# Two image streams in strict turn: the next image's first half moved beside the second attention

## The chip, the core and the metric

The kernel runs on one core of one Trainium2 chip. The metric is device time in microseconds: the median of three runs is 4172.8 (4169.99 to 4182.94).

## What is computed

A small vision transformer of two layers, on 64 images of 3 x 224 x 224. Each image becomes 196 patches of 16 x 16 and a class token, 197 tokens of 192 features.

```
h = tokens(x)                                   # patches @ W + b, class token, positions
h = h + attention0(layernorm(h))                # one head, 192 wide: q, k, v, softmax
h = h + ffn0(layernorm(h))                      # 3 experts; the image's mean token picks one (top 1)
h = h + attention1(layernorm(h))                # 12 heads of 16, output projection
h = h + ffn1(layernorm(h))                      # 191 tokens: 192 -> 768 -> gelu -> 192
                                                # first 6 tokens: gated experts ("atoms")
```

Everything is float32. Where the kernel uses the TensorE format fp32r it splits an operand into a high part and a remainder, so that a product of 192 features takes five matmuls.

## The kernel before, in words

**Streams and rounds.** Images go in pairs: stream 0 (A) takes the even image, stream 1 (B) the odd one. Each stream has its own half of PSUM, four banks (L260), and its own SBUF tiles. A round does one pair; there are 32 rounds, of which all but the ends are one hardware loop (`run_stages`, L405).

**Stages.** An image's work is a list of 58 named stages, `STAGES` (L69). In order: q0, v0, s0, p0, o0 (first attention: folded query and key, values, scores, transposed softmax, output), stat2, norm2, turn2 (normalisation: moments on VectorE, reciprocal root on POOL, applied on VectorE, transposed on TensorE, split by ScalarE and VectorE), route (expert's choice), hid0 and out0 (first FFN: three stages of products with gelu on ScalarE, two of output), a third normalisation, qk1 and v1, six max stages and maxT (row maxima of the 12 heads' scores), fourteen att stages (scores transposed, exponential, and at att5, att9 and att13 a group of four heads' output with its division on VectorE), proj, a fourth normalisation, hid1 and out1. The stages x, tok0, tok1 and the first normalisation (`AHEAD`, L68) are done for the next image, within the same list.

**Order.** `MERGE` (L80) is a string of 123 letters that says whose stage comes next: a, b, or r for a seventh part of POOL's regrouping of the pixels. It came from a search, and B begins at stage 38. `merged_order` (L84) makes the list `ORDER` of it. Every engine goes through the same list and takes its part of each stage (`stages` in each engine's block), so the list is the program order of all of TensorE, VectorE, ScalarE, POOL and SP (the DMA issues). Between engines there are semaphores.

**Around the change.** On SP, stage route loads the chosen expert (L473 to L489): W1 with remainders, 1188 KB, into `shared`, 384 KB into `w_last`, biases, and W2, 576 KB. `shared` later takes the stacked keys of the second attention, and qk1 fills it by DMA (L491). maxT sends the maxima by DMA into the stacks (L507). norm4 stores six tokens (L511), out1_1 stores the image from a tile `y` (L520). On TensorE, q0 and o0 use bank 2 of the stream, v0 and the outputs bank 3, s0 bank 0, p0 and route bank 1 (`TURN_BANK`, L106, says where a transposition goes). probs0 and the transposed `turned` lie in the ring of the second attention's exponentials (L231, L232), and the first attention's values in the tile `vals` of the second. `norm_count` (L398) counts the normalisations of a stream in their order.

On ScalarE, the exponentials (L1151, L1202, L1226) and the gelu (L1209) need different activation tables, and the compiler puts an ACT_TABLE_LOAD where the function changes.

Of the kernel before, what the change touches and what calls it, by code (L numbers as in the profile page):

```python
# [24 lines left out]
D = 192  # L25
# [21 lines left out]
RING = 6  # L47
STAGED = 2
# [12 lines left out]
def ffn_stages(n):  # L61
# [44 lines left out]
TURN_BANK = {1: 3, 2: 3, 3: 0, 4: 1}  # L106
# [3 lines left out]
def vit_kernel(nc, x, tok_w, tok_b, cls_tok, pos, attn_w, wg, w1, b1, w2, b2, w_qkv, w_proj, b_proj,  # L110
               fc1_w, fc1_b, fc2_w, fc2_b, gate_pair, atom_in_w, atom_in_b, atom_out_w, atom_out_b,
               balance, out, scratch):
    with ExitStack() as ctx:
# [52 lines left out]
        with ExitStack() as loop:  # L166
# [13 lines left out]
            w2_sb = two("w2_sb", [128, HC, D])  # L180
# [50 lines left out]
            probs0 = [probs[p][0][:, 0, :, :] for p in range(2)]  # L231
            turned = [probs[p][0][:, 1, :, :] for p in range(2)]  # L232
            y = two("y", [R, T, D])
# [164 lines left out]
        def norm_count(n, it):  # L398

            if n == 1:  # L400
                return 1 if isinstance(it, int) and it == 0 else 4 * it - 1
            last = isinstance(it, int) and it == PAIRS - 1
            return 4 * it + {2: 2, 3: 4 - last, 4: 5 - last}[n]
# [27 lines left out]
        def _(sp):  # L431
# [36 lines left out]
            def stages(name, p, it):  # L468
# [4 lines left out]
                if name == "route":  # L473

                    sp.wait_ge(expert_ready[p], it + 1)
# [44 lines left out]
                if name == "out1_1":  # L520
                    sp.wait_ge(out_ready[p], it + 1)
                    img = 2 * it + p
                    sp.dma_start(out[bass.ds(img, 1), NCLS:R].rearrange("o s d -> (o s) d"),
                                 y[p][NCLS - 1:R - 1, 0, :]).then_inc(stored[p], 16)
                    sp.dma_start(out[bass.ds(img, 1), R:SEQ].rearrange("o s d -> (o s) d"),
                                 y[p][0:R - 1, 1, :]).then_inc(stored[p], 16)
# [66 lines left out]
        def _(pe):  # L593
# [82 lines left out]
            def hidden(p, n, j, chunk):  # L676
                for c in (2 * j, 2 * j + 1):
                    last = accumulate(bank[p][HIDDEN_BANK[n][j]][:, (c % 2) * SP_:(c % 2 + 1) * SP_],
                                      swapped(products(tokens(p), chunk(c))))
                last.then_inc(hid_done[p], 1)  # L680
# [12 lines left out]
            def stages(name, p, it):  # L693
                b = bank[p]
                if name == "x":
                    if not isinstance(it, int) or it:
                        pe.wait_ge(logit_ready[0], it)
# [22 lines left out]
                elif name == "q0":  # L720
                    pe.wait_ge(xnT_ready[p], norm_count(1, it))
                    for m in range(2):
                        last = accumulate(b[2][:, m * SP_:(m + 1) * SP_], swapped(products(
                            tokens(p, None, tokT), columns(qk_fold, slice(m * 128, (m + 1) * 128)))))
                    last.then_inc(g_done[p], 1)
                elif name == "v0":
                    if not isinstance(it, int) or it:
                        pe.wait_ge(out_ready[p], it)
                    values(p, it, b[3], attn_wv, tokT)
                elif name == "s0":  # L730
                    pe.wait_ge(g_ready[p], it + 1)
                    for t in range(T):
                        last = accumulate(b[0][0:R, t * SP_:(t + 1) * SP_], swapped(products(
                            tokens(p, None, tokT), columns(xnT[p], slice(t * R, (t + 1) * R)))))
                    last.then_inc(s0_done[p], 1)
                elif name == "p0":
                    pe.wait_ge(p0_ready[p], it + 1)
                    for kt in range(T):
                        for t in range(T):
                            last = t_.transpose(b[1][0:R, kt * SP_ + t * R:kt * SP_ + (t + 1) * R],  # L740
                                                probs0[p][:, t, kt * R:(kt + 1) * R], ident[0:R, 0:R])
                    last.then_inc(p0_turned[p], 1)
                elif name == "o0":
                    pe.wait_ge(p0T_ready[p], it + 1)
                    pe.wait_ge(v_ready[p], 2 * it + 1)
                    for t in range(T):
                        last = accumulate(b[2][0:R, t * D:(t + 1) * D],
                                          [(turned[p][:, kt, t * R:(t + 1) * R], vals[p][:, kt, :, 0:HD])
                                           for kt in range(T)])
                    last.then_inc(o0_done[p], 1)  # L750
                elif name == "route":
                    pe.wait_ge(xsum_ready[p], it + 1)
                    accumulate(b[1][0:R, 0:EXPERTS],
# [7 lines left out]
                elif name[:4] == "out0":  # L761
                    if name == "out0_0":
                        pe.wait_ge(experts_loaded[p], 16 * it + 16)
                        if not (isinstance(it, int) and it == PAIRS - 1):
                            pe.wait_ge(xnT_ready[p], norm_count(1, it + 1))
# [8 lines left out]
                elif name == "v1":  # L774
                    values(p, it, b[0], v_wT, xnT)
                elif name[0] == "max":
                    j = name[1]
                    if j == 0:
                        pe.wait_ge(low_ready[p], 2 * it + 2)
                        pe.wait_ge(stacked[p], 144 * it + 144)  # L780
                        pe.wait_ge(v_ready[p], 2 * it + 2)
# [48 lines left out]
                elif name[:4] == "out1":  # L830
                    hid_out(p, it, 1, int(name[5]), fc2_wT, bias_pair[:, 1, :])
# [39 lines left out]
        def _(dve):  # L871
# [12 lines left out]
            for p in range(2):  # L884
                v.memset(probs0[p][:, :, SEQ:SP_], 0.0)
# [54 lines left out]
            def token_moments(p, it, n):  # L940
                dve.wait_ge(h_ready[p], norm_count(n, it))
                for t in range(T):
                    last = v.bn_stats(stats[p][:, t, :], (h_tok[p] if n == 1 else h_tiles[p])[:, t, :])  # L943
# [7 lines left out]
            def apply_norm(p, it, n):  # L951
                dve.wait_ge(rstd_ready[p], norm_count(n, it))
                for t in range(T):
                    for at, lo in ((0, 0), (D, 128)):
                        last = v.tensor_scalar(xn[p][:, t, at:at + D - lo], (h_tok[p] if n == 1 else h_tiles[p])[:, t, lo:D],  # L955
# [3 lines left out]
            def stages(name, p, it):  # L959
# [15 lines left out]
                elif name[:4] == "turn":  # L975

                    n = int(name[4])
                    dst = (tokT if n == 1 else xnT)[p]
# [6 lines left out]
                elif name == "q0":  # L985
# [4 lines left out]
                        in1=b[2][:, 0:2 * SP_], op0=ALU.mult, op1=ALU.add).then_inc(g_ready[p], 1)  # L990
# [275 lines left out]
```

## Time and profile before

| | us |
|---|---|
| median of 3 runs | 4172.8 |
| profiled execution | 4169.5 |
| its span, first to last instruction | 4167.7 |
| TensorE (PE) busy | 3189.7 (77%) |
| VectorE (DVE) busy | 2134.8 (51%) |
| ScalarE (ACT) busy | 1402.9 (34%) |
| POOL busy | 360.5 (9%) |
| granted TensorE clock, mean | 0.862 |

The chain that ended last goes 47% through PE, 29% through DVE, 8% through DMA, 5% through issue and 4% each through SP's queue and ACT. "Busy" is the sum of an engine's instructions; a clock of 1.0 is full speed. The time in brackets at a timeline row is idle time of that engine just before, with what ended it. A number x12 counts instructions that the view has merged; a float32 product counts as two.

### The profile page before, as it was taken

The page shows a single profiled execution, that of the slowest core. Times are in us where ns is not written, and L with a number is a line of the kernel's source. Part 1 is how long each engine was busy: PE and PEld are TensorE (multiplying, and loading weights), DVE is VectorE, ACT ScalarE, POOL GpSimd, SP SyncE. Part 2 cuts the span into 40 slices and gives each one's busy share as a digit, 9 for nine tenths or more (in the row PEclk, how much of TensorE's full clock was granted, in tenths as well). Part 3 has the DMA queues.
Part 4 walks back from the last instruction along what each step waited for, and adds up shares of the span by engine and source line. Part 5 has one row for each costly group of instructions (what it writes and reads, how often), then busy time and mean ns, then how long its engine had stood idle before and what let it go on. Part 6 is the DMA issues. An engine that isn't in the chain of part 4 may idle for free.

```text
span 4167.7 us, 63512 instructions
## 1 busy us (share of the span) xinstructions
PE 3189.7 (77%) x23190; PEld 2834.1 (68%) x23190; DVE 2134.8 (51%) x5288; ACT 1402.9 (34%) x2904; POOL 360.5 (9%) x746
## 2 busy tenths in 40 slices
PE   4777877777877777777777787777778777777757
PEld 3667766767766676776666776667677666677646
DVE  4555555554555555555555455554555555555433
ACT  2333333333333333333333333333333333333321
POOL 1000000010000000010001000010010000100000
PEclk9888888888988888888888898888888888889877
DMA  4332222332322333222233232223322223322221
GB/s 122 79 80 70 69 60 47 81 79 69 79 57 56 64 79 78 71 70 58 47 81 79 69 81 66 55 54 80 80 69 73 56 47 80 79 73 66 64 62 32
DMA packets 127223, 287.54 MB, mean 69 GB/s; under 512 B 28791, under 2 KB 95368, under 8 KB 116173
## 3 DMA queue, kind: packets, MB, share of 16 engines
q1 hardware_dynamic: 127180, 286.97, 29.7%
q8 instruction: 27, 0.44, 0.0%
q14 instruction: 16, 0.12, 0.0%
HBM read 192.23 MB, written 15.00 MB: 50 GB/s over the span
## 4 chain that ended last, share of the span: by engine, by line
PE 47%; DVE 29%; DMA 8%; issue 5%; SPq 4%; ACT 4%; POOL 3%; DVEq 0%; POOLq 0%; ACTq 0%
PE banks L640 21%; PE banks L687 8%; DVE inv L1061 5%; DVE hx L955 5%; PE banks L817 5%; DMA shared<-low 4%; DVE nmax L1050 4%; PE banks L786 4%; PE banks L804 3%; DMA shared<-nmaxT 3%; DVE stats L943 3%; POOL rstd L586 2%; PE banks L664 2%; DVE xnT L981 2%; DVE sums L1059 2%
## 5 line engine op out<-in xcount | busy, mean ns | idle before, releaser
L786 PE MATMUL banks<-shared,q_stack 128*99 128x198 f32 x1536 | 282.2, 336 | 238.4 <-issue 103.3
L1050 DVE TENSOR_REDUCE nmax<-banks 99x4 f32<-99x788 f32 x384 | 360.3, 974 | 155.8 <-PE banks L786 152.5
L786 PEld LDWEIGHTS banks<-shared,q_stack 128*99 128x99 f32 x1536 | 225.3, 225 | 292.3 <-issue 110.8
L640 PE MATMUL banks<-xnT,fc_wT 128*128 128x198 f32 x1920 | 359.3, 363 | 42.1 <-DVE xnT L981 42.1
L640 PEld LDWEIGHTS banks<-xnT,fc_wT 128*128 128x128 f32 x1920 | 346.0, 278 | 50.1 <-DVE xnT L981 50.0
L804 PE MATMUL banks<-q_stack,shared 128*99 128x198 f32 x1536 | 268.0, 301 | 140.1 <-DMA shared<-nmaxT 118.4
L1191 ACT ACTIVATE xnT<-banks 128x396 fp32r<-128x396 f32 x192 | 96.1, 501 | 820.6 <-PE banks L664 820.6
L584 POOL TENSOR_TENSOR var_eps<-moments,eps 99x2 f32<-99x2 f32 x256 | 51.1, 200 | 3642.2 <-DVE moments L948 3642.2
L804 PEld LDWEIGHTS banks<-q_stack,shared 128*99 128x99 f32 x1536 | 204.4, 194 | 203.6 <-DMA shared<-nmaxT 106.8
L687 PE MATMUL banks<-w_sb,hidT 128*99 128x192 f32 x1536 | 338.7, 383 | 0.0
L955 DVE TENSOR_SCALAR hx<-hx,moments,rstd 99x192 f32<-99x192 f32 (+1 forms) x768 | 248.0, 385 | 160.8 <-POOL rstd L586 157.2
L1226 ACT ACTIVATE probs_first<-banks 99x396 f32<-99x396 f32 x256 | 114.0, 497 | 616.2 <-PE banks L804 616.2
L687 PEld LDWEIGHTS banks<-w_sb,hidT 128*99 128x99 f32 x1536 | 293.2, 201 | 11.7
L687 PE MATMUL banks<-fc_wT,hidT 128*99 128x192 f32 x1536 | 273.0, 327 | 0.0
L640 PE MATMUL banks<-tok_wT,xT 128*99 128x192 f32 x1536 | 270.0, 330 | 3.5 <-ACT xT L1182 0.9
L1061 DVE RECIPROCAL inv<-sums 128x198 f32<-128x198 f32 x192 | 267.2, 1392 | 6.6
L817 PE MATMUL banks<-probs_rest,vals 99*32 99x198 f32 (+1 forms) x2048 | 186.7, 361 | 100.4 <-DVE headT L1063 65.5
L640 PEld LDWEIGHTS banks<-tok_wT,xT 128*99 128x99 f32 x1536 | 245.4, 168 | 8.9 <-issue 7.2
L1226 ACT ACTIVATE probs_rest<-banks 99x396 f32<-99x396 f32 x512 | 228.0, 497 | 64.6 <-PE banks L804 61.3
L687 PEld LDWEIGHTS banks<-fc_wT,hidT 128*99 128x99 f32 x1536 | 240.6, 166 | 0.5
L1209 ACT ACTIVATE hidT<-banks,fc_bc 128x198 f32<-128x198 f32 x384 | 142.5, 423 | 290.3 <-PE banks L640 290.3
L664 PE MATMUL banks<-ident,hx 99*128 99x99 f32 x1024 | 158.0, 284 | 106.2 <-DVE hx L955 103.9
(191 smaller groups left out, 5592.3 us busy)
## 6 DMA issues: line engine op xcount, KB each, us to landing
shared<-w_split SPq DMA_DIRECT2D x64, 1188.0 KB
xin<-in_x_dram SPq DMA_DIRECT2D x32, 1176.0 KB
w_sb<-in_L_ffn_W_dram SPq DMA_DIRECT2D x64, 576.0 KB, 6.2
w_last<-w_split SPq DMA_DIRECT2D x64, 384.0 KB
q_stack<-hi SPq DMA_DIRECT2D x128, 148.5 KB
q_stack<-low SPq DMA_DIRECT2D x128, 148.5 KB
shared<-hi SPq DMA_DIRECT2D x128, 148.5 KB
shared<-low SPq DMA_DIRECT2D x128, 148.5 KB
```

Source lines behind the costliest of these rows:

```text
L640: last = t_.matmul(dst, a, b, start=(j == 0), stop=(j == len(pairs) - 1))
L664: last = t_.transpose(b[:, k * SP_ + t * R:k * SP_ + (t + 1) * R], xn[p][:, t, k * 128:(k + 1) * 128], ident[0:R, 0:R])
L687: t_.matmul(b[0:R, t * D:(t + 1) * D], hidT[p][:, c, t * R:(t + 1) * R], w[:, c, :], start=(c == 0), stop=False)
L786: last = t_.matmul(b[n % 4][0:R, t * SP_:(t + 1) * SP_], q_stack[p][:, n, t * R:(t + 1) * R], k_stack[p][:, n, :], start=True, stop=True)
L804: last = t_.matmul(b[s % 2][0:R, kt * SP_:(kt + 1) * SP_], k_stack[p][:, s, kt * R:(kt + 1) * R], q_stack[p][:, s, :], start=True, stop=True)
L817: last = t_.matmul(b[2][r:r + 32, 0:SP_], vals[p][0:rows, kt, head(h), :], ring(p, h)[0:rows, kt, :], start=(kt == 0), stop=(kt == T - 1))
L943: last = v.bn_stats(stats[p][:, t, :], (h_tok[p] if n == 1 else h_tiles[p])[:, t, :])
L955: last = v.tensor_scalar(xn[p][:, t, at:at + D - lo], (h_tok[p] if n == 1 else h_tiles[p])[:, t, lo:D], moments[p][:, t, 0:1], rstd[p][:, ...
L1050: v.tensor_reduce(nmax1[p][:, :, 2 * j:2 * j + 2].rearrange("p t h -> p h t"), src, AX, ALU.max, negate=True).then_inc(nmax1_ready[p], 1)
L1061: v.reciprocal(inv1[p][:], sums1[p][:]).then_inc(inv1_ready[p], 1)
L1209: last = s_.activation(hidT[p][:, c, :], b[HIDDEN_BANK[layer][j]][:, (c % 2) * SP_:(c % 2 + 1) * SP_], ACT.Gelu, bias=bias[:, c:c + 1], sc ...
L1226: s_.activation(ring(p, s).rearrange("p k s -> p (k s)"), b[s % 2][0:R, 0:T * SP_], ACT.Exp).then_inc(p1_ready[p], 1)
```

## The change

The stages q0 to route of an image move into `AHEAD`: they are done for the next image, q0 and v0 ahead of the max stages and s0, p0, o0, the second normalisation and route between the att stages (`BESIDE`). The expert's load becomes a stage of its own, load, behind proj, since it overwrites `shared`. The order is no longer the searched one: A and B take turns stage by stage, and B begins at stage 28 of 57. The rest follows from that: h of the first half stays in `h_tok` until out0_1, probs0, `turned` and the values `vals0` get tiles of their own (in space of `w2_sb`), the image is stored from `h` in place of `y`, the first half uses bank 3 (v0 bank 1, the first transposition bank 0), the second half of keys takes 98 rows in place of 99, and waits guard what is shared.

```
-AHEAD = ["x", "tok0", "tok1"] + norm_stages(1)
-STAGES = (["q0", "v0", "s0", "p0", "o0"] + norm_stages(2)
-          + ["route", "x", "tok0", "tok1", "stat1", "split", "norm1", "hid0_0", "hid0_1", "turn1",
-             "hid0_2", "out0_0", "out0_1"] + norm_stages(3) + ["qk1_0", "qk1_1", "qk1_2", "v1"]
-          + [("max", j) for j in range(HEADS // 2)] + ["maxT"] + [("att", s) for s in range(HEADS + 2)]
-          + ["proj"] + norm_stages(4) + ffn_stages(1))
-B_FIRST = 38
-MERGE = ("bbbbbabbabbbbabbababbbabaababbbababaaabbaaabababararbaabrbabbbaabrbbarabbrbaaaaa"
-         "aaabaababaaaabaababaaabaaabbabbrabbabaabbab")
+AHEAD = (["x", "tok0", "tok1"] + norm_stages(1) + ["q0", "v0", "s0", "p0", "o0"] + norm_stages(2)
+         + ["route", "load"])
+BESIDE = {1: "s0", 3: "p0", 5: "o0", 7: "stat2", 8: "norm2", 9: "turn2", 11: "route"}
+ATTENTION = []
+for s in range(HEADS + 2):
+    ATTENTION += [("att", s)] + ([BESIDE[s]] if s in BESIDE else [])
+STAGES = (ffn_stages(0) + ["stat3", "x", "norm3", "tok0", "tok1", "turn3", "qk1_0", "qk1_1", "v1"]
+          + norm_stages(1) + ["q0", "v0"] + [("max", j) for j in range(HEADS // 2)] + ["maxT"] + ATTENTION
+          + ["proj", "load"] + norm_stages(4) + ffn_stages(1))
+B_FIRST = 28
+MERGE = ("ababababababababrababababababababrababababababababrababababababababarbababababab"
+         "ababarbabababababababarbababababababababr")
...
-TURN_BANK = {1: 3, 2: 3, 3: 0, 4: 1}
+TURN_BANK = {1: 0, 2: 3, 3: 1, 4: 1}
...
-                if name == "route":
+                if name == "load":
+                    if not isinstance(it, int) or it:
+                        sp.wait_ge(proj_done[p], it)
+                        sp.nop(nofuse=True)
                     sp.wait_ge(expert_ready[p], it + 1)
...
-                    if not isinstance(it, int) or it:
-                        pe.wait_ge(logit_ready[0], it)
...
                 elif name == "q0":
                     pe.wait_ge(xnT_ready[p], norm_count(1, it))
+                    if not isinstance(it, int) or it:
+                        pe.wait_ge(v_ready[p], 2 * it)
...
                 elif name == "v0":
                     if not isinstance(it, int) or it:
-                        pe.wait_ge(out_ready[p], it)
-                    values(p, it, b[3], attn_wv, tokT)
+                        pe.wait_ge(low_ready[p], 2 * it - 1)
+                    values(p, it, b[1], attn_wv, tokT)
...
                         pe.wait_ge(experts_loaded[p], 16 * it + 16)
-                        if not (isinstance(it, int) and it == PAIRS - 1):
-                            pe.wait_ge(xnT_ready[p], norm_count(1, it + 1))
+                        if isinstance(it, int) and it == 0:
+                            pe.wait_ge(logit_ready[p], 1)
+                        else:
+                            pe.wait_ge(out_ready[p], it)
...
                         pe.wait_ge(stacked[p], 144 * it + 144)
-                        pe.wait_ge(v_ready[p], 2 * it + 2)
+                        if isinstance(it, int) and it == PAIRS - 1:
+                            pe.wait_ge(v_ready[p], 2 * it + 2)
+                        else:
+                            pe.wait_ge(v_ready[p], 2 * it + 3)
+                            pe.wait_ge(g_ready[p], it + 2)
...
                 elif name[:4] == "out1":
+                    if name == "out1_0" and not (isinstance(it, int) and it == PAIRS - 1):
+                        pe.wait_ge(logit_ready[p], it + 2)
...
                 dve.wait_ge(rstd_ready[p], norm_count(n, it))
+                if not (n == 1 and isinstance(it, int) and it == 0):
+                    dve.wait_ge(xn_turned[p], norm_count(n, it) - 1)
...
                     dve.wait_ge(weight_ready[p], it + 1)
-                    v.scalar_tensor_tensor(out=h[p], in0=b[3][0:R, 0:T * D], scalar=weight[p][:, 0:1], in1=h[p],
+                    dve.wait_ge(stored[p], 32 * it + 32)
+                    v.scalar_tensor_tensor(out=h[p], in0=b[3][0:R, 0:T * D], scalar=weight[p][:, 0:1],
+                                           in1=h_tok[p][:].rearrange("p t d -> p (t d)"),
...
-                    dve.wait_ge(stored[p], 32 * it + 32)
-                    v.tensor_tensor(y[p][:].rearrange("p t d -> p (t d)"), b[3][0:R, 0:T * D], h[p],
+                    dve.wait_ge(cls_stored[p], 32 * it + 64)
+                    v.tensor_tensor(h[p], b[3][0:R, 0:T * D], h[p],
```

The new order of one round, as `merged_order` makes it (+1 is the next image, -1 the round before; the regroup parts are left out):

```
A:hid0_0 B:s0 A:hid0_1 B:att2-1 A:hid0_2 B:att3-1 A:out0_0 B:p0 A:out0_1 B:att4-1 A:stat3 B:att5-1 A:x+1 B:o0
A:norm3 B:att6-1 A:tok0+1 B:att7-1 A:tok1+1 B:stat2 A:turn3 B:att8-1 A:qk1_0 B:norm2 A:qk1_1 B:att9-1 A:v1
B:turn2 A:stat1+1 B:att10-1 A:norm1+1 B:att11-1 A:turn1+1 B:route A:q0+1 B:att12-1 A:v0+1 B:att13-1 A:max0
B:proj-1 A:max1 B:load A:max2 B:stat4-1 A:max3 B:norm4-1 A:max4 B:turn4-1 A:max5 B:hid1_0-1 A:maxT B:hid1_1-1
A:att0 B:hid1_2-1 A:att1 B:out1_0-1 A:s0+1 B:out1_1-1 A:att2 B:hid0_0 A:att3 B:hid0_1 A:p0+1 B:hid0_2 A:att4
B:out0_0 A:att5 B:out0_1 A:o0+1 B:stat3 A:att6 A:att7 B:norm3 A:stat2+1 B:tok0+1 A:att8 B:tok1+1 A:norm2+1
B:turn3 A:att9 B:qk1_0 A:turn2+1 B:qk1_1 A:att10 B:v1 A:att11 B:stat1+1 A:route+1 B:norm1+1 A:att12 B:turn1+1
A:att13 B:q0+1 A:proj B:v0+1 A:load+1 B:max0 A:stat4 B:max1 A:norm4 B:max2 A:turn4 B:max3 A:hid1_0 B:max4
A:hid1_1 B:max5 A:hid1_2 B:maxT A:out1_0 B:att0 A:out1_1 B:att1
```

## Rows read from the trace of the kernel before

**Rows 1.** The page: busy time, share of the span and instructions of each engine.
```profile
PE 3189.7 (77%) x23190; PEld 2834.1 (68%) x23190; DVE 2134.8 (51%) x5288; ACT 1402.9 (34%) x2904; POOL 360.5 (9%) x746
```

**Rows 2.** Timeline of VectorE: start us, us, instruction; stream A's tokens, two rounds.
```profile
1973.12 0.62 DVE L968 SCALAR_TENSOR_TENSOR h_tok<-banks,not_cls,pos_b 99x384 f32<-99x384 f32 x1 [1.31 <-PE banks L640]
...
2095.40 0.62 DVE L968 SCALAR_TENSOR_TENSOR h_tok<-banks,not_cls,pos_b 99x384 f32<-99x384 f32 x1 [1.31 <-PE banks L640]
```

**Rows 3.** Windows, one round: length, busy by engine, PE clock, DMA share, GB/s.
```profile
1910.00:2032.28 122.28, 95.98 (x706) 86.06 (x707) 63.71 (x162) 42.53 (x89) 11.12 (x23) 0.86 0.29 68
```

**Rows 4.** Windows, same columns: a dense stretch, and the maxima of stream A.
```profile
1986.90:2005.90 19.00, 17.41 (x133) 16.77 (x131) 8.51 (x24) 6.96 (x13) 4.03 (x8) 1.00 0.62 154
2009.20:2024.40 15.20, 9.56 (x54) 7.52 (x58) 8.53 (x17) 3.06 (x7) 0.88 (x2) 0.56 0.01 1
```

**Rows 5.** Timeline of TensorE: first maxima product, and first score of the attention.
```profile
2009.25 0.98 PE L786 MATMUL banks<-shared,q_stack 128*99 128x198 f32 x8 [3.24 <-DMA shared<-low]
...
2019.91 0.99 PE L804 MATMUL banks<-q_stack,shared 128*99 128x198 f32 x4 [3.38 <-DMA shared<-nmaxT]
```

**Rows 6.** Timeline of TensorE: q0, and two output stages of an FFN.
```profile
1934.82 1.28 PE L640 MATMUL banks<-tokT,qk_fold 128*128 128x198 f32 x10
...
1982.75 4.16 PE L687 MATMUL banks<-w_sb,hidT 128*99 128x192 f32 x12
...
1986.87 2.18 PE L687 MATMUL banks<-w_sb,hidT 128*99 128x192 f32 x12
```

**Rows 7.** Groups by line of ScalarE: xcount, busy us, mean ns, idle before.
```profile
L1226 ACT ACTIVATE probs_rest<-banks 99x396 f32<-99x396 f32 x512 | 228.0, 497 | 64.6 <-PE banks L804 61.3
L1209 ACT ACT_TABLE_LOAD x128 | 164.2, 1283 | 2.2
L1209 ACT ACTIVATE hidT<-banks,fc_bc 128x198 f32<-128x198 f32 x384 | 142.5, 423 | 290.3 <-PE banks L640 290.3
...
L1226 ACT ACT_TABLE_LOAD x64 | 82.1, 1283 | 1.1
L1202 ACT ACT_TABLE_LOAD x63 | 80.8, 1283 | 1.1
```

**Rows 8.** Groups by line of VectorE: row maxima and a head group's three steps.
```profile
L1050 DVE TENSOR_REDUCE nmax<-banks 99x4 f32<-99x788 f32 x384 | 360.3, 974 | 155.8 <-PE banks L786 152.5
L1061 DVE RECIPROCAL inv<-sums 128x198 f32<-128x198 f32 x192 | 267.2, 1392 | 6.6
...
L1059 DVE STREAM_SHUFFLE sums<-banks 128x198 f32<-128x198 f32 x192 | 74.6, 389 | 1.7
L1063 DVE TENSOR_TENSOR headT<-banks,inv 128x198 f32<-128x198 f32 x192 | 70.0, 365 | 6.5
```

**Rows 9.** Timeline of VectorE: a normalisation, and the cast of the maxima.
```profile
1913.94 0.62 DVE L943 BATCH_NORM_STATS2 stats<-hx 99x6 f32<-99x192 f32 x2
...
1915.99 1.38 DVE L955 TENSOR_SCALAR hx<-hx,moments,rstd 99x192 f32<-99x192 f32 x4 [1.07 <-POOL rstd L586]
...
2016.57 0.35 DVE L1054 CAST nmaxT<-banks 24x198 fp32r<-24x198 f32 x1 [0.68 <-PE banks L792]
```

**Rows 10.** Timeline of SP's queue: the second stream's expert load is issued.
```profile
1984.62 0.38 SPq L483 DMA_DIRECT2D shared<-w_split  x1
```

**Rows 11.** Timeline of TensorE: the first product that reads this load.
```profile
1997.12 0.61 PE L640 MATMUL banks<-xnT,shared 128*128 128x198 f32 x4
```

**Rows 12.** Timeline of TensorE at the start: q0 of the first image.
```profile
93.84 2.44 PE L640 MATMUL banks<-tokT,qk_fold 128*128 128x198 f32 x10
```

**Rows 13.** Timeline of VectorE at the start: the first image's expert is known.
```profile
113.46 0.15 DVE L1025 SCALAR_TENSOR_TENSOR expert<-below 1x1 int32<-1x1 f32 x1
```

**Rows 14.** Timeline of ScalarE: activation, table load, activation.
```profile
1997.32 0.50 ACT L1215 ACTIVATE hi<-banks 96x396 fp32r<-96x396 f32 x1 [0.43 <-PE banks L640]
1997.83 1.28 ACT L1209 ACT_TABLE_LOAD   x1
1999.12 1.37 ACT L1209 ACTIVATE hidT<-banks,b_sb 128x198 f32<-128x198 f32 x4
```

More of the change, by code:

```diff
@@ L47 @@
 RING = 6
+ROUTED = 448
 STAGED = 2
@@ L179, in vit_kernel @@
                                 for s in (k_stack, q_stack)]
-            w2_sb = two("w2_sb", [128, HC, D])
+            w2_sb, vals0, probs0, turned = [], [], [], []
+            for p in range(2):
+                with ExitStack() as weights:
+                    w2_sb.append(sb(f"w2_sb{p}", [128, HC, D], stack=weights))
+                vals0.append(sb(f"vals0{p}", [R, T, D], stack=loop))
+                probs0.append(sb(f"probs0{p}", [R, T, SP_], stack=loop))
+                turned.append(sb(f"turned{p}", [R, T, SP_], stack=loop))
             xnT = two("xnT", [128, 2, 2, SP_], F32R)
@@ L737, in stages @@
                     pe.wait_ge(p0_ready[p], it + 1)
-                    for kt in range(T):
+                    for kt, keys in ((0, R), (1, SEQ - R)):
                         for t in range(T):
-                            last = t_.transpose(b[1][0:R, kt * SP_ + t * R:kt * SP_ + (t + 1) * R],
-                                                probs0[p][:, t, kt * R:(kt + 1) * R], ident[0:R, 0:R])
+                            last = t_.transpose(b[3][0:keys, kt * SP_ + t * R:kt * SP_ + (t + 1) * R],
+                                                probs0[p][:, t, kt * R:kt * R + keys], ident[0:R, 0:R])
                     last.then_inc(p0_turned[p], 1)
@@ L746, in stages @@
                     for t in range(T):
-                        last = accumulate(b[2][0:R, t * D:(t + 1) * D],
-                                          [(turned[p][:, kt, t * R:(t + 1) * R], vals[p][:, kt, :, 0:HD])
-                                           for kt in range(T)])
+                        last = accumulate(b[3][0:R, t * D:(t + 1) * D],
+                                          [(turned[p][0:keys, kt, t * R:(t + 1) * R], vals0[p][0:keys, kt, :])
+                                           for kt, keys in ((0, R), (1, SEQ - R))])
                     last.then_inc(o0_done[p], 1)
@@ L942, in token_moments @@
                 for t in range(T):
-                    last = v.bn_stats(stats[p][:, t, :], (h_tok[p] if n == 1 else h_tiles[p])[:, t, :])
+                    last = v.bn_stats(stats[p][:, t, :], norm_source(p, n)[:, t, :])
                 last.then_inc(stats_ready[p], 1)
@@ L1002, in stages @@
                     dve.wait_ge(inv0_ready[p], it + 1)
-                    if not (isinstance(it, int) and it == 0):
-                        dve.wait_ge(out_ready[p], it)
-                    dve.wait_ge(cls_stored[p], 32 * it + 32)
                     for t in range(T):
-                        last = v.scalar_tensor_tensor(out=h_tiles[p][:, t, :], in0=b[2][0:R, t * D:(t + 1) * D],
+                        last = v.scalar_tensor_tensor(out=h_tok[p][:, t, :], in0=b[3][0:R, t * D:(t + 1) * D],
                                                       scalar=inv0[p][:, t:t + 1], in1=h_tok[p][:, t, :],
```

56 lines of the change are left out of this document (30 added, 26 removed).

## The prediction

> **What bounds the kernel now.** Read the page's busy shares first: TensorE (PE) works 77% of the span, VectorE 51%, ScalarE 34% [rows 1]. No engine is full, so the time is a chain of waits. The VectorE timeline then gives the repeat: the same h_tok row starts at 1973.12 and at 2095.40, one round of two images in 122.28 us [rows 2], and 32 rounds make almost all of the span. The windows view of one such round shows 95.98 us of PE busy, so 26.3 us of PE idle, at a granted clock of 0.86 [rows 3]. A mean of 0.86 between the two levels 1.0 (2.4 GHz) and 0.5 (1.2 GHz) means that some 28% of the round, 34 us, runs at the low one. The rows show where: 19 us of dense work (17.41 busy) stand at 1.00; the stretch from 2009.2, entered after 3.24 us without work, stands at 0.56 over 15.2 us [rows 4, 5]. What it costs is seen on one stage: twelve product passes take 4.16 us at the low level and 2.18 at the high one [rows 6].
>
> **What the change does to the chain.** It takes q0 to route out of the chain of an image and puts them beside the attention of the image before. It also replaces the searched order by strict turns, half a round apart. Since every engine takes its stages in the one order list, a late stage holds everything behind it on its own engine. So I price a round by walking the new list: each stage begins when its engine and what it awaits are done. Durations: ten TensorE products 1.1 to 1.3 us, an FFN output stage 2.1 to 2.2 (high clock) [rows 6]; an exp 0.50, two gelus 0.8, a table load 1.28 [rows 7]; a head group on VectorE 0.39+1.39+0.37, 2.2 with gaps; a maximum 0.97 [rows 8]; a normalisation about 1.0 for statistics, 1.07 waiting for POOL, 1.1 to 1.4 to apply [rows 9]; other VectorE steps 0.35 to 0.75. The maxima's way through DMA costs 3.0 (cast of nmaxT ended at 2016.92, first product at 2019.91) [rows 5, 9].
>
> **ScalarE's tables.** Before, 255 loads, 8 a round [rows 7]. Following the new list through ScalarE, exp and gelu change places 16 times a round, because one stream's hid0 and hid1 now stand between the other's exponentials. That is 8 more loads, 10.3 us a round. A load runs ahead of its data where ScalarE idles, but in strict turn it does not idle there.
>
> **First half** (from stream B's first scores, att0, to A's), high clock throughout:
> (a) 14.35 us to A's out0_0. ScalarE decides: after att1's exp at 3.35 come load, gelus hid0_0, load, s0's softmax (0.9), load, gelus hid0_1, load, exp att2, load, gelus hid0_2: 13.5, then the last third of out0_0.
> (b) 16.85 to A's normalised input: p0, out0_1 and att5's heads on PE (to 18.3), head group on VectorE behind out0_1 and stat3 (to 20.8), x copies (23.3), o0 (25.1), norm3, then tok0 and tok1 on PE (28.95), tok add, stat2, turn3 (31.2).
> (c) 18.8 to the third head group: qk1 with its two remainders, norm2 and the second head group on VectorE (37.55), turn2, stat1, POOL, norm1 (41.6), turn1 across three engines (43.45), route's sum, q0, v0, heads (47.8), head group (50.0).
> (d) 12.05 to the cast of the maxima: proj 2.4, its add, then VectorE alternates maxima with stat4, norm4, turn4 to 61.0; maxT and cast.
> (e) 3.05 through DMA. Sum 65.1.
>
> **Second half** (A's att0 to B's): (a) 15.75: att0's exp, load and hid1_2's gelus, the rest of out1_0 (4.0), s0 and out1_1 (7.15) bring att2's scores to 7.7; then ScalarE has exp, load, gelus, load, exp, load and two pairs of gelus, to 14.85. The last third of out0_0 follows. (b) 12.65, on VectorE after att5's heads at 17.0: head group (19.2), out0_1's add, o0 (21.1), stat3, POOL, norm3 (24.4), stat2, tok add (26.0), POOL, norm2 (27.7), turn3 (28.4). (c) 12.95, all VectorE: head group (30.6), two remainders and turn2 (32.4), stat1 (33.4), route (35.95), norm1 (37.3), turn1 (39.15), head group (41.35). (d) 16.1: proj (43.5) stands ahead of v0 and its copy (45.25), so the first maximum is ready for VectorE at 46.0; maxima, stat4, norm4 and turn4 alternate to 52.15; then hid1 stands between the maxima on PE, to 56.6; maxT and cast 57.45. (e) 3.05. Sum 60.5.
>
> The round at the high clock is thus 125.6 us, already 3.3 above the present one, though the present one includes 34 us at the low level. The walk also leaves PE gaps of 1.8 to 5 us: before out0_0 (3.2), norm1 (5.1), around route (2.8), in both maxima phases, before both att0. Before, gaps like 3.24 us led into low stretches [rows 5]; these will too.
>
> **The clock's term.** Work on the walk's path inside such stretches, which takes up to twice as long: out0_1 and heads in the first half 2.5; turn1, route, q0, v0 and heads 3.5; proj, turn4 and hid1_0 3; in the second half out1_0 and s0 3; proj and v0 2; hid1 between maxima 2: 16 in all. Bounds: 0, if dense work keeps 1.00 throughout as in [rows 4]; 20, if all these stages take what the row at 4.16 shows. I take 11, two thirds of the 16: the maxima phase, which stays in kind, does stand at 0.56 now [rows 4], but dense work brings the clock back, as where the stage of 4.16 is followed at once by one of 2.18 [rows 6]. Round: 136.6.
>
> **Edits with one answer.** The load of the expert now waits for proj and stands in SP's queue ahead of norm4's two stores and the other stream's nmaxT copies. Its five issues are over long before those copies are ready (load at 52.4, copies at 62). Its 2.1 MB may still hold them up by 0 to 2 us in the first half; I take 0. The weights themselves have over 20 us until hid0_0; now the second stream's load, issued at 1984.62, is first read at 1997.12 without a wait [rows 10, 11], so 12.5 us are enough. If that cover went, the same 12.5 us less what is left would show before hid0_0. The added waits (q0 for v1's copy, v0 for the remainder, out0_0 for out_ready or logits, out1_0 for the route, apply for the earlier turn, stores before overwriting h) are met several stages earlier; only max0's wait for v0's copy bites, 0.65, in (d), and PE's stages behind it wait too. Bank moves, own buffers for probs0 and vals0, and 98 keys instead of 99 cost nothing: same instructions, same counts. The regroup parts on POOL (7 a round) may delay a rstd by one copy: 0 to 0.6, taken as 0.
>
> **Ends.** The start now runs two first halves one after the other; the first takes from q0 at 93.84 to the expert's index at 113.46, 20 us [rows 12, 13]. The first round has no attention of B and the last no next image, which gives about as much back: 0, bounds -30 and +30.
>
> **Sum.** The profiled execution took 4169.5 us (span 4167.7), 0.1% under the median of 4172.8. The first image pair starts the pattern, so 31 repeats change: 31 x (136.6 - 122.28) = 444. 4169.5 + 444 = **4613 us**, 10.6% more.
>
> **A rule against the rows.** ScalarE's rows show the load starting 0.01 us after the activation before it and the next activation starting as it ends [rows 14], so I count 1.28. The Trainium skill (ScalarE: Activation LUTs, What ACT_TABLE_LOAD costs) adds a drain of 1.38 us to each switch, 2.66 in all; by that page the eight loads on the walk's path would lengthen a round by 11 us and the time, as an estimate, to about 4954. The trace does not agree: no such gap stands at this load. The page's rule to batch calls by set (Table sets: the hidden batching unit) speaks against strict turns, and the trace agrees in that each switch does take 1283 ns.
>
> **Rivals.**
> (1) *The clock holds.* Gaps are short and many, and the work between them keeps PE at 1.00, as the dense stretch does. Then the round is 125.6 to 129 and the time 4272 to 4380. For it: a granted 1.00 over 19 us with 1.6 us idle [rows 4]. Against: the gaps of 3 us and more in the walk. 0.18.
> (2) *Faster: the shorter chain wins.* Place: q0 to route no longer precedes hid0, and the other stream's work fills the waits. If PE were then held up only by the two DMA ways of the maxima and the head groups, the round were its 95.98 busy plus 6 (twice 3.0) and 10 (six head groups of 2.2, a quarter of it filled), 112 us, and the time 4169.5 - 31 x 10.3 = 3850. It decides once idle PE falls under the present 26.3 us a round [rows 3]. For it: PE is the busiest engine and a third of an image's chain is removed. Against: strict turn lets ScalarE's loads and VectorE's order hold PE, and the walk is longer than the present round even at the high clock. 0.10, and 0.02 for a net of nothing.
> (3) *A switch costs more.* Place: the eight loads on the walk's path, five in (a) of the first half and three in (a) of the second. If each held ScalarE for twice its 1.28, because the engine empties first when exponentials and gelus stand back to back, a round were 10.3 us longer and the time 4932. Against: no gap around the load now [rows 14]. 0.05. The drain that the Trainium skill's page on ScalarE states would do this.
> That the change does not do what it says has no room: the list is fixed.
>
> **Numbers.** My forecast, 4613 with 4380 to 4890 around it (round 129 to 145.6), has 0.65. The range takes in rival 1 down to 4260 and the clock's upper bound up to 4890. A difference within 0.3%, about what a measurement of this kernel can tell from no change, gets 0.02. Faster 0.10, slower 0.88.
>
> **What would show it.** Right: a repeat near 137 us; about 510 table loads; granted clock near 0.75 to 0.8; PE's busy share near 70%; idle PE before out0_0 ended by ScalarE's gelu, before turn1 by VectorE; VectorE and DMA longer in the chain of waits. Wrong: a repeat under 122, or loads hidden behind idle ScalarE, or a clock at 0.86 or more.

## The result, and the profile after

The changed kernel takes 4726.2 us (median of 4 runs, 4720.8 to 4729.3) beside 4174.8 us for the kernel before in the same set of runs: ratio 1.1317, 95% interval 1.1296 to 1.1339. The forecast was 4613 us, within 4260 to 4890.

The page after, busy shares, granted clock and chain of waits, answers to [rows 1]:

```profile
span 4723.4 us, 64430 instructions
...
PE 3420.3 (72%) x23190; PEld 3068.4 (65%) x23190; DVE 2070.7 (44%) x5286; ACT 1751.1 (37%) x3154; POOL 360.4 (8%) x746
...
PE 48%; DVE 24%; ACT 11%; issue 8%; DMA 3%; POOL 3%; SPq 2%; DVEq 0%; ACTq 0%; POOLq 0%
```

The instructions are as many, yet PE is busy 3420 us in place of the 3190 of [rows 1]: its clock was granted lower, 0.80 for 0.86. The share falls all the same, because idle time grew more.

The repeat, from the VectorE timeline (start, us, instruction), and that round in the windows view (columns as in [rows 3]):

```profile
2096.47 0.62 DVE L994 SCALAR_TENSOR_TENSOR h_tok<-banks,not_cls,pos_b 99x384 f32<-99x384 f32 x1 [2.78 <-PE banks L656]
...
2236.40 0.62 DVE L994 SCALAR_TENSOR_TENSOR h_tok<-banks,not_cls,pos_b 99x384 f32<-99x384 f32 x1 [2.79 <-PE banks L656]
```
```profile
2064.00:2203.93 139.93, 102.63 (x708) 92.64 (x708) 62.38 (x161) 54.02 (x97) 11.10 (x23) 0.80 0.27 60
```

A round grew from 122.28 to 139.93 us, by 17.65 [rows 2]. [Rows 3] had 95.98 busy on PE and 26.3 idle; now it is 102.63 and 37.3. So 6.65 us of the 17.65 are the same PE work at a lower clock (0.80 for 0.86), and 11.0 are PE idle. Times 31 rounds that is 547 of the span's 555.7 us more; start and end make the other 8.5.

Where the idle stands, from the groups of PE by line (last columns: idle before, and what ended it), first in the kernel before, then in the changed one:

```profile
L687 PE MATMUL banks<-w_sb,hidT 128*99 128x192 f32 x1536 | 338.7, 383 | 0.0
...
L664 PE MATMUL banks<-ident,hx 99*128 99x99 f32 x1024 | 158.0, 284 | 106.2 <-DVE hx L955 103.9
```
```profile
L704 PE MATMUL banks<-w_sb,hidT 128*99 128x192 f32 x1536 | 361.1, 385 | 201.4 <-ACT hidT L1234 201.4
...
L680 PE MATMUL banks<-ident,hx 99*128 99x99 f32 x1024 | 175.2, 306 | 434.1 <-DVE hx L981 434.1
```

And ScalarE's table loads in the changed kernel:

```profile
L1234 ACT ACT_TABLE_LOAD x253 | 324.6, 1283 | 4.4
...
L1251 ACT ACT_TABLE_LOAD x221 | 283.5, 1283 | 3.9
...
L1176 ACT ACT_TABLE_LOAD x31 | 39.8, 1283 | 0.6
```

The first FFN's output stages wait 201 us for gelus, where they waited for none, and the transposes wait 434 us for VectorE's normalised rows, where they waited 106. These two groups gained 529 us of idle, while PE's idle in all grew by 325: other waits shrank, the one before the maxima's products from 238 to 88. Loads went from 255 [rows 7] to 505, some 16 a round. How they come to stand in front of out0_0 is seen on ScalarE, then on PE:

```profile
2066.76 0.50 ACT L1251 ACTIVATE probs_first<-banks 99x396 f32<-99x396 f32 x1 [1.72 <-PE banks L827]
2067.28 1.28 ACT L1234 ACT_TABLE_LOAD   x1
2068.57 0.74 ACT L1234 ACTIVATE hidT<-banks,b_sb 128x198 f32<-128x198 f32 x2
2069.34 1.28 ACT L1176 ACT_TABLE_LOAD   x1
...
2073.63 1.28 ACT L1251 ACT_TABLE_LOAD   x1
2074.92 0.50 ACT L1251 ACTIVATE probs_rest<-banks 99x396 f32<-99x396 f32 x1
2075.44 1.28 ACT L1234 ACT_TABLE_LOAD   x1
2076.74 0.74 ACT L1234 ACTIVATE hidT<-banks,b_sb 128x198 f32<-128x198 f32 x2
```
```profile
2073.66 0.89 PE L704 MATMUL banks<-w_sb,hidT 128*99 128x192 f32 x4 [1.64 <-ACT hidT L1234]
2077.53 1.60 PE L704 MATMUL banks<-w_sb,hidT 128*99 128x192 f32 x4 [2.97 <-ACT hidT L1234]
```

From 2066.76 to 2079.3 ScalarE never idles: one exponential of one stream, a load, two gelus of the other, a load, and so on. The second and the last third of out0_0 on PE, shown here, each start right behind their pair of gelus.

### The profile page after: what moved, and what is told of

It reads as the page before. It is cut to its first block, busy times and chain, and to the rows that moved or that the text cites. A ratio compares the mean times of both kernels' runs of the same rounds, so it can differ in the third digit from the quotient of the medians.

```text
span 4723.4 us, 64430 instructions
## 1 busy us (share of the span) xinstructions
PE 3420.3 (72%) x23190; PEld 3068.4 (65%) x23190; DVE 2070.7 (44%) x5286; ACT 1751.1 (37%) x3154; POOL 360.4 (8%) x746
## 4 chain that ended last, share of the span: by engine, by line
PE 48%; DVE 24%; ACT 11%; issue 8%; DMA 3%; POOL 3%; SPq 2%; DVEq 0%; ACTq 0%; POOLq 0%
PE banks L656 26%; PE banks L704 11%; DVE hx L981 5%; DVE inv L1086 4%; ACT L1234 3%; DVE stats L967 3%; DMA shared<-nmaxT 3%; PE banks L680 2%; POOL rstd L602 2%; PE banks L840 2%; ACT hidT L1234 2%; ACT L1251 2%; PE banks L827 2%; DVE xnT L1007 2%; DVE moments L972 1%
## 5 line engine op out<-in xcount | busy, mean ns | idle before, releaser
L656 PE MATMUL banks<-tokT,fc_wT 128*128 128x198 f32 x1920 | 411.3, 389 | 43.0 <-DVE tokT L1007 43.0
L680 PEld LDWEIGHTS banks<-ident,hx 99*128 99x128 f32 x1024 | 126.1, 170 | 457.2 <-DVE hx L981 455.9
L656 PEld LDWEIGHTS banks<-tokT,fc_wT 128*128 128x128 f32 x1920 | 384.3, 300 | 58.8 <-DVE tokT L1007 58.8
L1216 ACT ACTIVATE tokT<-banks 128x396 fp32r<-128x396 f32 x128 | 64.1, 501 | 898.0 <-PE banks L680 898.0
L827 PE MATMUL banks<-q_stack,shared 128*99 128x198 f32 x1536 | 302.3, 292 | 90.1 <-DMA shared<-nmaxT 88.6
L1234 ACT ACT_TABLE_LOAD x253 | 324.6, 1283 | 4.4
L704 PE MATMUL banks<-fc_wT,hidT 128*99 128x192 f32 x1536 | 313.3, 361 | 0.9 <-ACT hidT L1234 0.9
L809 PE MATMUL banks<-shared,q_stack 128*99 128x198 f32 x1536 | 248.2, 299 | 88.1 <-DVE nmax L1075 55.6
L656 PE MATMUL banks<-proj_wT,headT 128*99 128x192 f32 x768 | 251.8, 498 | 63.4 <-DVE headT L1088 62.0
L1251 ACT ACT_TABLE_LOAD x221 | 283.5, 1283 | 3.9
L704 PEld LDWEIGHTS banks<-fc_wT,hidT 128*99 128x99 f32 x1536 | 277.4, 190 | 9.4 <-ACT hidT L1234 1.5
L809 PEld LDWEIGHTS banks<-shared,q_stack 128*99 128x99 f32 x1536 | 200.3, 198 | 120.3 <-DVE nmax L1075 72.8
```

Of the source, the lines that this page charges most:

```text
L656: last = t_.matmul(dst, a, b, start=(j == 0), stop=(j == len(pairs) - 1))
L680: last = t_.transpose(b[:, k * SP_ + t * R:k * SP_ + (t + 1) * R], xn[p][:, t, k * 128:(k + 1) * 128], ident[0:R, 0:R])
L704: t_.matmul(b[0:R, t * D:(t + 1) * D], hidT[p][:, c, t * R:(t + 1) * R], w[:, c, :], start=(c == 0), stop=False)
L809: last = t_.matmul(b[n % 4][0:R, t * SP_:(t + 1) * SP_], q_stack[p][:, n, t * R:(t + 1) * R], k_stack[p][:, n, :], start=True, stop=True)
L827: last = t_.matmul(b[s % 2][0:R, kt * SP_:(kt + 1) * SP_], k_stack[p][:, s, kt * R:(kt + 1) * R], q_stack[p][:, s, :], start=True, stop=True)
L1234: last = s_.activation(hidT[p][:, c, :], b[HIDDEN_BANK[layer][j]][:, (c % 2) * SP_:(c % 2 + 1) * SP_], ACT.Gelu, bias=bias[:, c:c + 1], sc ...
```

## The experiments

Each ratio is to the kernel before, run on the same chip beside it. The kernels of experiments 2, 3 and 10 put Exp in the place of Gelu inside the loop, so the gelu itself is left out there; the count and size of ScalarE's activations stay the same, and so does their mean length in that line (423 to 427 ns).

**1. The gelus together.** ScalarE alone gets an order of its own, in which a stream's gelu stages follow each other instead of standing between the other's exponentials:

```
+for stage, before in ((("hid0_1", 0), ("s0", 1)), (("hid0_2", 0), ("s0", 1)), (("hid1_2", 1), (("att", 0), 0)),
+                      (("hid0_1", 1), (("att", 3), 0)), (("hid0_2", 1), (("att", 3), 0))):
+    ACT_ORDER = moved(ACT_ORDER, stage, before)
...
-            run_stages(act, stages)
+            run_stages(act, stages, ACT_ORDER)
```


> ScalarE alone takes its stages in another order: the three gelu stages of a hidden layer stand together, ahead of the other stream's exponentials; every other engine keeps the strict turns. Table loads fall from 16 to 8 a round. Theory (loads between one stream's gelus and the other's exponentials hold out0_0): the waits before out0_0 of 4.6 and 1.8 us a round shrink, a round is 5 to 10 us shorter, time 4420 to 4570. Rival (the turn order on the other engines decides, the loads only fill time that another wait would take): less than 2 us a round, time 4660 to 4740.

Measured 4567.3 us, ratio 1.0940 [1.0906, 1.0975]. Its groups show 255 loads again, and no wait before the first FFN's output stages:

```profile
L1246 ACT ACT_TABLE_LOAD x128 | 164.2, 1283 | 2.2
...
L1263 ACT ACT_TABLE_LOAD x96 | 123.2, 1283 | 1.7
...
L1188 ACT ACT_TABLE_LOAD x31 | 39.8, 1283 | 0.6
```
```profile
L716 PE MATMUL banks<-w_sb,hidT 128*99 128x192 f32 x1536 | 273.1, 328 | 0.0
```
With half the loads gone, 159 us of the 551 lost came back, while the granted clock fell to 0.79. ScalarE's order changed together with the number of loads, so this run does not part the two; experiment 2 does.

**2. One table, changed kernel.** `ACT.Gelu` becomes `ACT.Exp` in line 1234, and no load is left in the loop.

> The changed kernel with exp computed in place of gelu in both hidden layers of the image loop, so that no table changes hands there. Left out: the gelu itself. Theory: as with the gelus together and somewhat more, since the order on ScalarE stays that of the turns, 7 to 12 us a round, time 4350 to 4510. Rival: under 2 us a round, time above 4660.

Measured 4404.4 us, ratio 1.0553 [1.0521, 1.0586]: 322 us less, or 10.4 a round. The idle before the first FFN's output stages is gone, that before the transposes is not:

```profile
PE 3294.1 (75%) x23190; PEld 2988.7 (68%) x23190; DVE 2068.8 (47%) x5286; ACT 1085.8 (25%) x2650; POOL 359.7 (8%) x746
...
L704 PE MATMUL banks<-w_sb,hidT 128*99 128x192 f32 x1536 | 273.1, 327 | 0.0
...
L680 PE MATMUL banks<-ident,hx 99*128 99x99 f32 x1024 | 160.6, 287 | 433.6 <-DVE hx L981 433.6
```
Of the 322 us, 195 are idle time of PE and 126 are PE's busy time (3420.3 to 3294.1), at a granted clock of 0.82 for 0.80.

**3. One table, kernel before.** The same edit in the kernel before (its line 1209).

> The kernel before with exp in place of gelu in the image loop (the gelu is left out), the control for the one above. Theory: its 8 loads a round run ahead of their data while ScalarE idles, so under 1.5 us a round, time 4125 to 4180. Rival (a load costs wherever it stands): 8 loads of 1.28 us, 10 us a round, time near 3860.

Measured 4174.2 us, ratio 1.0000 [0.9985, 1.0016]. The 255 loads of before cost nothing that this measurement can tell. In the round of [rows 3], ScalarE idles behind six of the eight loads; two, that of [rows 14] among them, stand right between activations, but the output stages behind the gelus do not wait (0.0 in line 687 above).

**4. Strict turns alone.** The stages of before, its letters replaced by strict alternation, half a round apart:

```
-B_FIRST = 38
+B_FIRST = 29
-MERGE = ("bbbbbabbabbbbabbababbbabaababbbababaaabbaaabababararbaabrbabbbaabrbbarabbrbaaaaa"
...
+MERGE = "ababababababababrababababababababrababababababababrabababab...
```


> One part of the change alone: the kernel before with its own stages, in strict turns and half a round apart (B begins at stage 29 of 58). Theory (strict turns are what costs): slower than before by 5 to 20%, 4380 to 5000. Rival (moving the first half beside the attention is what costs): within 2% of before, 4090 to 4260.

Measured 5049.0 us, ratio 1.2096 [1.2059, 1.2132], beyond the upper end. Strict turns alone cost more than the whole change, and putting the first half beside the second attention went with a shorter time, 5049 to 4726. By itself this pair does not show a gain of the move, since the stages meet others in the two lists (experiment 7); experiments 5 and 9 together do.

**5. The same list, searched turns.** The changed kernel, its offset of 28 kept; only the letters differ, chosen by a search over the program's waits:

```
 B_FIRST = 28
-MERGE = ("ababababababababrababababababababrababababababababrababababababababarbababababab"
-         "ababarbabababababababarbababababababababr")
+MERGE = ("aaabaabababbbbbbbaabbaabbaabbbbbaaabbrbabaabraababaababbbabbbaaabrabaaraaabaraa"
+         "bbaabbaababaaaabbbabaabrabbbabbabbaabaabrb")
```


> The changed kernel with its stages, banks and offset of 28 turns as they are; only the letters of the merge differ: 114 turns and 7 regroups in an order that a search of the waits chose, not in strict alternation. Theory (the strict turns are what costs: each stream's chain waits behind stages of the other that are not ready, and moving the first half beside the second attention is a gain by itself, as strict 5048.97 against strict 4726 says): the round falls below the 122.28 us of before, so 3500 to 4150 us, clock above 0.86. Rival (the longer chain through the second attention is what costs, whatever the turns): 4500 to 4750 us. Between them (4150 to 4500) both have a share.

Measured **3473.5 us, ratio 0.8319 [0.8291, 0.8346]**: a quarter less than strict turns, and faster than both kernels. Its page:

```profile
PE 2956.3 (85%) x23190; PEld 2702.1 (78%) x23190; DVE 2064.7 (59%) x5286; ACT 1334.4 (38%) x2840; POOL 361.9 (10%) x746
...
PE 63%; DVE 26%; issue 4%; ACT 3%; POOL 2%; DMA 1%; SPq 1%; DVEq 0%; POOLq 0%; ACTq 0%
...
L704 PE MATMUL banks<-w_sb,hidT 128*99 128x192 f32 x1536 | 267.9, 326 | 0.0
...
L680 PE MATMUL banks<-ident,hx 99*128 99x99 f32 x1024 | 157.2, 283 | 69.9 <-DVE hx L981 69.9
```
and two of its rounds in the windows view (columns as in [rows 3]):

```profile
1934.34:2037.21 102.87, 91.81 (x707) 84.42 (x706) 62.54 (x162) 40.92 (x87) 11.15 (x23) 0.87 0.37 82
2037.21:2136.83 99.62, 88.29 (x714) 81.30 (x712) 62.19 (x162) 40.74 (x87) 11.14 (x23) 0.91 0.38 84
```
The mean round is 101.2 us. Against the strict order's 139.93, PE idle falls by 26.1 (37.3 to 11.2) and PE's busy time by 12.6 (102.63 to a mean of 90.05). VectorE's busy time is the same. The two waits of the changed kernel fall from 201 and 434 us to 0 and 70, and the chain of waits now runs through PE for 63%.

**6. Another offset, searched.** As 5, with an offset of 41 turns and letters searched for it.

> The same list of stages with an offset of 41 turns and letters searched for it. Theory (turns, not the place of the streams, set the time): within 4% of the searched order at 28 turns, 3500 to 4150 us. Rival (half a round is a bad place for the streams and that is where the time went): this one is over 5% faster than the searched order at 28 turns.

Measured 3519.4 us, ratio 0.8429 [0.8413, 0.8444], 1.3% above experiment 5. Half a round apart is no bad place by itself.

**7. Another offset, strict.** `B_FIRST` 36 for 28 in the changed kernel, nothing else.

> The changed kernel with strict turns kept and the second stream started 36 turns after the first in place of 28: each stage stands beside another stage of the other image. Theory (in a strict order it is chance which stage stands in front of which, and 28 is a middling place): the time moves by over 3% with the offset alone, 4150 to 4550 us. Rival (strict turns cost the same wherever the streams stand): 4600 to 4850 us.

Measured 4248.2 us, ratio 1.0176 [1.0158, 1.0194]: 478 us less than at 28. Its groups:

```profile
L704 PE MATMUL banks<-w_sb,hidT 128*99 128x192 f32 x1536 | 275.7, 327 | 68.2 <-ACT hidT L1234 68.2
...
L680 PE MATMUL banks<-ident,hx 99*128 99x99 f32 x1024 | 167.8, 296 | 325.8 <-DVE hx L981 325.7
```
Loads in lines 1234 and 1251 fall from 474 to 317 and both waits shrink. In strict alternation the offset decides which stage stands in front of which, and of the two tried 28 is the unlucky one.

**8. Filling PE's gaps.** Spare matmuls (128 rows, 112 columns, results read by nobody) before the transposes of normalisations 1 and 4 and between the thirds of out0_0:

```
+            def fill(p, k, count):
+                for _ in range(count):
+                    t_.matmul(bank[p][k][:, 2 * SP_:2 * SP_ + 112], fc1_wT[:, 0, 0, 0:128], fc1_wT[:, 0, 0, 0:112],
+                              start=True, stop=True)
...
+                if n == 1 and not (isinstance(it, int) and it == 0):
+                    pe.wait_ge(low_ready[p], 2 * it)
+                    fill(p, 2, 60 if p == 0 else 30)
+                if n == 4:
+                    fill(p, 2, 36)
...
+                    if n == 0 and t == 0 and c in (2, 4):
+                        fill(p, 1, 20 * (c - 2) + (20 if c == 2 else 0) if p == 0 else 20)
```


> The changed kernel with spare matmuls added on TensorE (results go to columns that nothing reads) in front of the waits where it stood idle longest: before the transposes of the first and the fourth normalisation and between the first chunks of out0_0. Theory (TensorE is at its lower clock behind these gaps, and that is most of the 14.3 us of the repeat that the walk at the high clock lacks): the granted clock rises from 0.80 to 0.83 or more and the time falls although work is added, to 4470 to 4640 us. Rival (the low clock stands beside waits and off the path): 4720 to 4880 us.

Measured 4926.5 us, ratio 1.1812 [1.1785, 1.1839], above both ranges, although the clock rose to 0.88. Then a third of the fill (20 and 10, 12, 6, 12 and 7):

> The fill of the fourth kernel of the last set cut to about a third. There a spare matmul took 288 ns, not the 120 it was sized by, so 8294 of them were 1048.7 us, more than the gaps held; the clock rose to 0.88, yet the time rose by 200. Now 20 and 10 before the first normalisation's transposes, 12 before the fourth's, 6, 12, 7 and 7 between the chunks of out0_0: 86 in a round, 24.8 us, which fit into the gaps. Clock theory: the clock rises to about 0.84 and the time falls to 4520 to 4680 us. Rival (the low clock stands off the path, or the fill delays as much as the clock gives back): 4700 to 4850 us.

Measured 4730.0 us, ratio 1.1332 [1.1313, 1.1351], at a clock of 0.815: the time of the changed kernel, as the rival had it. Busy shares and fill rows, of the large fill and then of the small one, for which the two waits are shown too:

```profile
PE 4143.5 (84%) x31484; PEld 3857.5 (78%) x31484; DVE 2071.8 (42%) x5286; ACT 1758.2 (36%) x3154; POOL 360.5 (7%) x746
...
L678 PE MATMUL banks<-fc_wT 128*128 128x112 f32 x8294 | 1048.7, 288 | 0.3 <-DVE low L1078 0.3
```
```profile
PE 3714.8 (79%) x25912; PEld 3383.3 (72%) x25912; DVE 2069.6 (44%) x5286; ACT 1751.4 (37%) x3154; POOL 359.2 (8%) x746
...
L716 PE MATMUL banks<-w_sb,hidT 128*99 128x192 f32 x1536 | 350.5, 372 | 118.7 <-ACT hidT L1246 118.7
...
L678 PE MATMUL banks<-fc_wT 128*128 128x112 f32 x2722 | 381.6, 291 | 0.3 <-DVE low L1078 0.3
...
L690 PE MATMUL banks<-ident,hx 99*128 99x99 f32 x1024 | 171.1, 302 | 214.2 <-DVE hx L993 214.2
```
The second expectation misread the row of the large fill. Its 288 ns is the mean length of one matmul, which overlaps the next; the busy time is 1048.7/8294 = 126 ns each. So the large fill was sized about right per matmul but put 1049 us where the two waits had 635, and the small one put 12.3 us into a round, not 24.8.

PE's work other than fill fell from 3420 to 3095 us (4143.5 - 1048.7) with the large fill, and to 3333 with the small one. So the low clock does lengthen PE's work: at 0.88 in place of 0.80 it takes 325 us less, or 10.5 a round. But with the small fill the 87 us gained were met by 79 us of fill that outlasted the gaps (381.6 put in, idle before the same two groups down from 635.5 to 332.9). The fall in time did not come. These two runs leave open how much of the low clock lies on the path; the chain of waits gives an estimate in the next section.

**9. The search on the old list.** The kernel before with its own stages and offset of 38, letters chosen by the same search:

> The kernel before with its own list of stages and offset of 38 turns, letters chosen by the same search that gave 3473.5 on the changed list. Theory (the gain of that kernel comes from the list, with the first half beside the second attention, which leaves the search more to fill with): this one stays within 4% of before, 4000 to 4250 us. Rival (the search is simply better than the one behind the order of before): 3450 to 3800 us.

Measured 4170.0 us, ratio 0.9984 [0.9974, 0.9993]. At this offset the search finds 0.2% in the old list, so the gain of experiment 5 needs the changed kernel: its list, with the banks and buffers that go with it. No run parts these, and none searches the old list at another offset. The page shows something else too:

```profile
PE 3325.9 (80%) x23190; PEld 2943.0 (71%) x23190; DVE 2139.5 (51%) x5288; ACT 1414.6 (34%) x2904; POOL 363.4 (9%) x746
```
PE is 136 us longer at work than in [rows 1], at a mean clock of 0.823 for 0.862, and the time is the same within 0.2%.

**10. One table in the searched order.** Experiment 5 with the edit of 2.

> The searched order at 28 turns (3473.5 us, 193 table loads in the loop's three lines, against 505 in the changed kernel) with Exp in the place of Gelu in the loop, so that those loads go. Theory (a load costs only where ScalarE is what the next stage waits for; in this order they stand where it is idle): 3420 to 3490 us. Rival (each load costs what it cost in the strict order, 4726 less 4404 over 505 loads, 0.64 us): 3330 to 3370 us.

Measured 3473.4 us, ratio 0.8294 [0.8277, 0.8311], beside 0.8319 [0.8291, 0.8346] with its loads (191 in the three lines; the 193 above counts two outside the loop). The intervals overlap: between their outer ends the loads cost 0.15 us each, between their middles 0.05, against 0.64 each in strict order.

## Why the prediction was right

The forecast, its sign and its mechanism held; the time came 113 us above it. The walk can be held against the trace block by block, from B's att0 to A's and back, in the windows view (the granted clock stands third from the end):

```profile
2064.09:2079.09 15.00, 10.38 (x75) 9.63 (x75) 1.13 (x2) 12.65 (x20) 0.00 (x0) 0.87 0.38 90
2079.09:2098.59 19.50, 15.39 (x110) 14.03 (x108) 10.26 (x27) 5.39 (x10) 1.97 (x5) 0.84 0.00 0
2098.59:2119.47 20.88, 12.13 (x104) 10.36 (x105) 11.82 (x36) 4.93 (x12) 1.86 (x4) 0.75 0.46 59
2119.47:2134.72 15.25, 10.52 (x53) 9.44 (x54) 9.21 (x18) 2.46 (x4) 2.04 (x4) 0.73 0.41 145
2134.72:2137.73 3.01, 1.75 (x10) 1.51 (x9) 0.00 (x1) 1.27 (x4) 0.00 (x0) 0.50 0.03 6
2137.73:2155.41 17.68, 15.89 (x103) 15.24 (x104) 1.77 (x4) 13.89 (x23) 0.00 (x0) 0.84 0.03 8
2155.41:2167.93 12.52, 10.47 (x93) 9.39 (x91) 8.62 (x28) 3.59 (x8) 2.33 (x5) 1.00 0.00 0
2167.93:2180.68 12.75, 9.09 (x72) 7.46 (x72) 9.76 (x29) 3.54 (x9) 1.45 (x3) 0.75 0.75 96
2180.68:2200.94 20.26, 15.35 (x89) 14.15 (x89) 9.82 (x20) 4.96 (x10) 1.45 (x3) 0.74 0.30 109
2200.94:2204.03 3.09, 1.65 (x11) 1.44 (x10) 0.00 (x1) 1.33 (x2) 0.00 (x0) 1.00 0.02 6
```

The letters are the walk's.

- **The walk.** First half, measured and walked: (a) 15.00 for 14.35, (b) 19.50 for 16.85, (c) 20.88 for 18.8, (d) 15.25 for 12.05, (e) 3.01 for 3.05. Second half: 17.68 for 15.75, 12.52 for 12.65, 12.75 for 12.95, 20.26 for 16.1, 3.09 for 3.05. The block at a clock of 1.00, (b) of the second half, is met within 0.13. Block (c) behind it was walked as "all VectorE"; it took no longer than walked, but its chain of waits does go through PE, with four transposes (0.92) and a group's heads (1.52) at the low clock, so there the walk was about 1 us long elsewhere.
- **The clock's term** is the step that was mis-sized. The round exceeds the walk of 125.6 by 14.3, all of it in blocks at 0.73 to 0.87. The list of stages gave 16; I cut it to 11 because dense work was to bring the clock back. The cut was too deep: 3.3 us a round, 103 of the 113 us. The trace shows the same work on the path at both levels, as with the ten products of a third of hid1, first at 0.50 (2.45 us), then at 1.00 (1.25 us), in the windows view:

```profile
2131.55:2134.00 2.45, 2.45 (x12) 2.45 (x13) 0.83 (x1) 0.52 (x1) 0.00 (x0) 0.50 0.18 72
2198.95:2200.20 1.25, 1.25 (x13) 1.12 (x11) 0.98 (x1) 0.55 (x2) 0.00 (x0) 1.00 0.00 0
```
Set stage by stage against the same work at a clock of 1.00, in this trace and in those of before and of experiments 2 and 5, PE's pieces of this round's chain of waits are some 18 us longer (an estimate): in the first half 0.8, 3.1, 2.8 and 3.1 in (a) to (d), in the second 2.8, 0, 1.1 and 4.3. It is largest where the walk is exceeded most, and enough for all 14.3. No run takes the low clock away and nothing else, so the time that it costs is not measured.
- **The loads.** About 510 were forecast and 505 came. The count on the path held: five loads from 2067.28 to 2075.44 and three from 2147.98 to 2151.85 stand in front of the last gelus of the two out0_0. Eight at 1.28 make 10.3 us a round, and taking all loads out gave back 10.4, but that the two numbers meet is in part luck. The two blocks (a) of experiment 2 show it:

```profile
2056.88:2066.03 9.15, 9.15 (x74) 9.15 (x75) 1.13 (x2) 4.72 (x14) 0.00 (x0) 1.00 0.42 99
2123.21:2138.98 15.77, 15.77 (x103) 15.49 (x104) 1.77 (x4) 6.07 (x17) 0.00 (x0) 0.81 0.03 9
```
They took 15.00 and 17.68 with loads, so the blocks that hold the eight loads gave back 7.8 us and not 10.3: without loads PE is busy all through them and sets their length. The other 2.5 came mostly from block (b) of the first half, which fell from 19.50 to 18.01 at a clock of 0.91 for 0.84.
- **Rival 3 and the Trainium skill's rule.** The load at 2067.28 starts 0.02 us after the exponential ends, and the gelus start as it ends. Rival 3 would have needed a round 10.3 us longer than forecast; it was 3.3 longer. The Trainium skill (ScalarE: Activation LUTs, What ACT_TABLE_LOAD costs) puts a drain on each switch; the trace shows none, before or after.
- **Rival 1**, the clock holds, falls: 0.80. Of **rival 2** the place was right and the condition was not met: idle PE rose from 26.3 to 37.3 a round. Experiment 5 meets it, with 11.2 idle and 90 busy, and there the moved half gains 17%. Its 3850 stayed above the 3473 because it kept 16 us of waits and PE's 95.98 at the old clock.
- **The load of the expert** ahead of the maxima's copies: taken as 0, and the way from the end of the cast to att0 is 3.0 and 3.1, beside 3.0 before. **Ends**: taken as 0, measured 8.5.
- **What would show it.** PE's share of 72%, the gelus before out0_0 and VectorE before the transposes came as said. That VectorE and DMA would be longer in the chain did not: VectorE and DMA fell to 24% and 3%, and ScalarE rose to 11%.

## What to carry to other kernels

A change that moves work and also rewrites the order is two changes; price and test them apart. Here the move took 17% off the time with a fitting order, and with strict turns it added 13%. Count a table load by who waits for the activation behind it: here it cost nothing that could be measured where PE did not wait for it, and 0.64 us on average, of a length of 1.28, where PE waited behind half of the loads.

## What was not expected of the hardware

- A mean granted clock does not tell the time: 0.823 and 0.86 gave 4170 and 4178 us on the old list, and 0.88 went with 4926 us for the filled kernel against 0.80 with 4726.
- The mean length of a pipelined matmul is no price: 288 ns in the row of the spare matmuls, 126 ns of busy time each.
- 505 loads of 1283 ns cost 322 us in one order, and 191 of them nothing clear of the noise in another.
